# Vision tower on one core: the channel sums taken in two pieces a tile (three and four runs) instead of three (two, two, three), with the step tables laid out anew

## The reference

```
pooled = x.reshape(64, 12, 14, 16, 14, 16).sum(axis=(3, 5))
h = einsum('bcij,ce->bije', pooled, channel_weights)      # (64, 196, 192)
h = h + attn(layernorm(h))                                # one head of width 192
h = h + ffn(layernorm(h))                                 # 192 -> 768, gelu (tanh) -> 192
```

## Time and profile before

| | us |
|---|---|
| median of three runs | 494.9 (493.6 to 494.9) |
| the profiled execution | 494.9, of which span of the instructions 492.8 |
| PE busy | 425.7 |
| DVE busy | 381.7 (77% of the span) |
| ACT busy, POOL busy | 287.8, 255.0 |
| sums of pieces of two runs (96) and of three (48) | 190.4, 141.5 |

### The profile page before, as it was taken

How to read it: one execution, slowest core, us unless ns; L and a number is a source line. 1 busy time by engine, 2 the same in 40 slices (tenths; PEclk the granted TensorE clock), 3 DMA queues, 4 the chain that set the end, 5 groups by cost and what they waited for, 6 DMA issues and landing times.

```text
span 492.8 us, 10971 instructions
## 1 busy us (share of the span) xinstructions
PE 425.7 (86%) x4558; PEld 362.9 (74%) x4558; DVE 381.7 (77%) x288; ACT 287.8 (58%) x494; POOL 255.0 (52%) x194
## 2 busy tenths in 40 slices
PE   5976453996899999899898989798999899999996
PEld 4544232784678888788787978687888779888896
DVE  1788898899799998899989898989898999420000
ACT  1022044534878676758583858575868466877821
POOL 1032313703659293818374758475656657485940
PEclk9999555696699999989998999999999989999999
DMA  8999999999999999999999999999999997101101
GB/s 241 335 404 401 404 402 402 403 402 406 402 401 401 403 403 403 403 399 404 397 403 398 404 395 400 396 401 402 397 403 399 400 391 310 34 26 33 43 26 50
DMA packets 56661, 166.65 MB, mean 338 GB/s; under 512 B 5972, under 2 KB 13030, under 8 KB 56612
## 3 DMA queue, kind: packets, MB, share of 16 engines
q1 hardware_dynamic: 56612, 165.95, 87.7%
HBM read 156.29 MB, written 9.63 MB: 337 GB/s over the span
## 4 chain that ended last, share of the span: by engine, by line
DMA 47%; DVE 20%; PE 17%; SPq 7%; issue 4%; POOL 3%; ACT 1%; DVEq 0%; ACTq 0%
DMA xs<-x 47%; DVE pooled L480 18%; PE ps L609 17%; SPq L412 5%; POOL h_lo L1123 2%; DVE phat_tok L498 1%; POOL inv L1100 0%; POOL inv L1114 0%; ACT probs L967 0%; ACT out_sb L1024 0%; PE ps L786 0%; SPq L429 0%; DVE prod L489 0%; ACT h_hi L1018 0%; DVEq L475 0%
## 5 line engine op out<-in xcount | busy, mean ns | idle before, releaser
L480 DVE TENSOR_REDUCE pooled<-xs 128x28 f32<-128x1792 f32 x144 | 328.8, 2323 | 29.3 <-DMA xs<-x 29.3
L1123 POOL TENSOR_TENSOR h_lo<-h_f,h_hi 128x784 fp32r<-128x784 f32 x96 | 176.9, 1868 | 86.6 <-ACT h_hi L1018 86.6
L609 PE MATMUL ps<-w_hi,h_hi 128*98 128x192 f32 x768 | 207.9, 271 | 1.3 <-POOL h_lo L1123 1.1
L609 PE MATMUL ps<-w_lo,h_hi 128*98 128x192 f32 x768 | 196.9, 256 | 0.0
L609 PE MATMUL ps<-w_hi,h_lo 128*98 128x192 f32 x768 | 196.7, 256 | 0.0
L609 PEld LDWEIGHTS ps<-w_hi,h_hi 128*98 128x98 f32 x768 | 128.9, 168 | 16.7 <-issue 14.2
L609 PEld LDWEIGHTS ps<-w_lo,h_hi 128*98 128x98 f32 x768 | 129.4, 168 | 0.0
L609 PEld LDWEIGHTS ps<-w_hi,h_lo 128*98 128x98 f32 x768 | 129.1, 168 | 0.0
L1009 ACT ACTIVATE h_f<-ps 128x784 f32<-128x784 f32 x96 | 74.8, 824 | 21.7 <-PE ps L609 21.6
L1018 ACT CAST h_hi<-h_f 128x784 fp32r<-128x784 f32 x96 | 79.5, 851 | 0.1
L1100 POOL TENSOR_TENSOR inv<-var,minus_half 98x8 f32<-98x8 f32 x16 | 26.2, 1636 | 70.4 <-DVE var L494 70.3
(11 more groups left out here) (119 smaller groups left out, 355.4 us busy)
## 6 DMA issues: line engine op xcount, KB each, us to landing
xs<-x SPq DMA_DIRECT2D x336, 448.0 KB, 12.4
out<-out_sb SPq DMA_DIRECT2D x32, 294.0 KB
rows_sb<-wfc SPq DMA_DIRECT2D x1, 576.0 KB, 5.5
out_sb<-wproj SPq DMA_DIRECT2D x1, 576.0 KB, 10.4
h_f<-wqkv SPq DMA_DIRECT2D x1, 432.0 KB
cf<-const_full SPq DMA_DIRECT2D x1, 264.0 KB, 3.0
h_f<-const_paired SPq DMA_DIRECT2D x1, 153.0 KB, 3.3
cr<-const_rows SPq DMA_DIRECT2D x1, 83.2 KB
```

Of the source, the lines that this page charges most:

```text
L480: dve.tensor_reduce(pooled[:, n % 2, t, GRID * first:GRID * end].rearrange("p (i j) -> p i j", j=GRID), runs, AX.XY, ALU.add).then_inc(red ...
L609: return pe.matmul(o, a, b, start=start, stop=stop, skip_group_check=shared)
L1123: pool.tensor_tensor(h_lo[:, m % 2, t], h_f32[:, t], h_hi[:, m % 2, t].bitcast(F32), ALU.subtract).then_inc(h_lo_ready, 1)
```

## The change

The piece list has two entries instead of three. What depends on it follows: the number of pieces a group is six, DVE has 96 sums of `pooled` instead of 144, and the ring is given back in threes and fours.

```diff
-CHUNKS = ((0, 2), (2, 4), (4, 7))
+CHUNKS = ((0, 3), (3, 7))
 PER_TILE = len(CHUNKS)
 PER_GROUP = TILES * PER_TILE
...
 PERIOD = 254
-STEPS = 4910
+STEPS = 4938
...
-    "sum_rows": (443, 398, 375, 382, 391, 389, 367, 357, 353, 347, 337, 326, 316, 319, 313, 327),
+    "sum_rows": (365, 352, 347, 345, 333, 334, 365, 337, 341, 338, 326, 317, 311, 312, 334, 326),
...
 SETUP_AT = {
-    "pe_resid": 335, "pe_f": (389, 416), "pe_w1": (457, 494),
-    "act_f": 447, "act_w1": (476, 505), "dve_resid": 383,
-    "pool_wproj": 385, "pool_w1": 517,
+    "pe_resid": 335, "pe_f": (393, 420), "pe_w1": (462, 498),
+    "act_f": 452, "act_w1": (480, 510), "dve_resid": 387,
+    "pool_wproj": 385, "pool_w1": 522,
 }
```

More of the change, by code:

```diff
@@ L70 @@
 PERIOD = 254
-STEPS = 4910
+STEPS = 4938
 PE_ORDER = {
-    "sum_rows": (443, 398, 375, 382, 391, 389, 367, 357, 353, 347, 337, 326, 316, 319, 313, 327),
[L74 to L82, removed]
+    "sum_rows": (365, 352, 347, 345, 333, 334, 365, 337, 341, 338, 326, 317, 311, 312, 334, 326),
+    "turn_phat": (447, 420, 492, 431, 423, 414, 446, 394, 411, 392, 383, 375, 366, 365, 398, 408),
+    "apply_a": (476, 433, 505, 455, 489, 488, 508, 513, 491, 502, 494, 485, 477, 416, 421, 464),
+    "scores": (505, 564, 519, 543, 559, 553, 568, 553, 551, 542, 534, 525, 539, 510, 478, 480),
+    "turn_maxima": (567, 647, 646, 637, 604, 625, 609, 621, 611, 603, 594, 585, 588, 549, 544, 520),
+    "turned_scores": (581, 683, 659, 652, 618, 641, 639, 635, 627, 618, 609, 601, 602, 563, 570, 534),
+    "weigh": (613, 719, 700, 686, 650, 682, 671, 669, 660, 652, 643, 634, 633, 599, 637, 565),
+    "turn_context": (633, 744, 734, 715, 730, 709, 705, 692, 694, 686, 677, 669, 662, 630, 660, 598),
+    "turn_u": (647, 814, 772, 761, 753, 758, 764, 742, 744, 735, 727, 718, 701, 672, 687, 616),
+    "apply_g2": (660, 827, 823, 775, 778, 785, 781, 768, 770, 762, 753, 745, 726, 690, 705, 640),
@@ L83 @@
     "residual": (
-        (724, 850, 1043, 1039, 1028, 1022, 1018, 1008, 998, 987, 972, 961, 939, 930, 903, 838),
-        (1000, 1163, 1159, 1155, 1149, 1145, 1134, 1124, 1113, 1103, 1089, 1080, 1040, 1050, 1007, 923),
+        (665, 832, 1047, 1053, 1031, 1027, 1014, 1016, 1007, 999, 990, 998, 1000, 964, 949, 884),
+        (906, 1136, 1182, 1160, 1159, 1134, 1146, 1137, 1128, 1120, 1119, 1129, 1094, 1097, 1053, 969),
     ),
-    "turn_uhat": (784, 865, 821, 798, 799, 810, 799, 790, 779, 752, 747, 738, 716, 735, 704, 645),
+    "turn_uhat": (702, 885, 873, 838, 854, 836, 860, 836, 827, 819, 810, 802, 783, 741, 754, 691),
@@ L120 @@
 ACT_ORDER = {
[L121 to L125, removed]
+    "load_exp": (360, 574, 458, 560, 556, 546, 573, 558, 556, 548, 539, 530, 510, 514, 465, 478),
@@ L126 @@
+    "copy_p_tok": (375, 372, 357, 377, 365, 344, 375, 347, 351, 348, 336, 327, 321, 322, 358, 361),
+    "copy_phat": (460, 428, 499, 450, 442, 426, 459, 429, 425, 417, 408, 400, 376, 377, 410, 434),
+    "copy_b": (496, 442, 514, 537, 545, 543, 562, 547, 545, 536, 528, 519, 534, 426, 433, 474),
+    "copy_maxima": (576, 656, 654, 646, 613, 634, 618, 630, 620, 612, 603, 594, 597, 558, 553, 528),
     "exponentials": (
-        (609, 711, 655, 609, 603, 604, 605, 601, 584, 574, 563, 552, 532, 526, 535, 499),
@@ L128 @@
-        (617, 719, 663, 617, 611, 612, 613, 609, 592, 582, 571, 560, 540, 534, 543, 507),
-    ),
[L130 to L134, removed]
@@ L135 @@
-    "gelu": (
[6 rows of a table removed]
+        (595, 696, 673, 665, 632, 654, 652, 648, 640, 631, 623, 614, 615, 576, 584, 547),
+        (603, 704, 681, 673, 640, 662, 660, 656, 648, 639, 631, 622, 623, 584, 592, 555),
+    ),
+    "load_gelu": (611, 943, 935, 902, 924, 922, 918, 910, 901, 893, 887, 888, 851, 854, 817, 733),
+    "copy_context": (628, 732, 723, 700, 724, 695, 686, 682, 674, 665, 657, 648, 649, 619, 652, 587),
+    "copy_u": (654, 821, 810, 770, 762, 775, 776, 758, 758, 749, 740, 732, 720, 684, 699, 624),
@@ L142 @@
+    "keep_u": (658, 825, 829, 781, 774, 794, 788, 777, 769, 760, 752, 743, 732, 690, 707, 628),
+    "copy_uhat": (710, 892, 880, 846, 861, 844, 868, 843, 835, 826, 818, 809, 791, 752, 763, 703),
+    "gelu": (
[6 rows of a table added]
     ),
     "round_high": (
[6 rows of a table removed]
[6 rows of a table added]
     ),
     "take_out": (
[4 rows of a table removed]
[4 rows of a table added]
     ),
@@ L159 @@
     "reduce": (
[9 rows of a table removed]
[6 rows of a table added]
     ),
-    "variance1": (486, 416, 428, 421, 413, 440, 398, 420, 412, 404, 368, 362, 354, 355, 358, 346),
+    "variance1": (391, 380, 460, 399, 387, 375, 405, 353, 371, 355, 343, 335, 328, 329, 362, 365),
     "maxima": (
-        (561, 663, 538, 558, 550, 543, 535, 527, 520, 512, 507, 499, 475, 476, 477, 443),
-        (571, 673, 548, 568, 560, 552, 545, 537, 529, 522, 517, 509, 484, 485, 486, 453),
-    ),
-    "context": (695, 787, 710, 673, 659, 687, 679, 671, 664, 657, 651, 614, 604, 607, 614, 557),
-    "variance2": (750, 831, 784, 747, 740, 762, 754, 746, 739, 704, 696, 689, 670, 691, 656, 611),
+        (546, 597, 604, 592, 580, 572, 588, 576, 590, 578, 569, 563, 564, 523, 520, 493),
+        (556, 636, 614, 602, 590, 582, 598, 586, 600, 588, 579, 572, 573, 533, 530, 503),
+    ),
+    "context": (640, 807, 765, 753, 742, 716, 749, 699, 712, 700, 692, 687, 688, 661, 666, 604),
+    "variance2": (668, 851, 839, 788, 818, 796, 822, 798, 786, 774, 766, 767, 739, 698, 714, 648),
 }
 POOL_ORDER = {
-    "scale_p": (493, 423, 442, 428, 438, 457, 405, 437, 433, 421, 376, 369, 362, 371, 372, 362),
-    "scale_u": (760, 841, 796, 771, 771, 781, 769, 765, 753, 727, 720, 713, 684, 704, 676, 621),
+    "scale_p": (419, 387, 467, 406, 394, 382, 413, 361, 378, 363, 351, 342, 336, 337, 370, 373),
+    "scale_u": (678, 860, 848, 809, 828, 809, 833, 811, 803, 794, 786, 777, 756, 708, 723, 658),
     "low_part": (
[6 rows of a table removed]
[6 rows of a table added]
     ),
@@ L191 @@
     "load": (
[9 rows of a table removed]
[6 rows of a table added]
     ),
     "send": (
-        (1089, 1254, 1247, 1246, 1226, 1223, 1225, 1215, 1204, 1194, 1174, 1168, 1131, 1140, 1098, 1014),
-        (1195, 1388, 1379, 1369, 1363, 1359, 1349, 1339, 1328, 1317, 1302, 1284, 1275, 1245, 1183, 1099),
+        (976, 1209, 1255, 1233, 1231, 1207, 1219, 1210, 1201, 1193, 1190, 1202, 1162, 1170, 1126, 1042),
+        (1082, 1374, 1380, 1358, 1351, 1341, 1341, 1332, 1323, 1315, 1325, 1327, 1290, 1274, 1211, 1127),
     ),
```

## The result

The changed kernel takes 499.25 us (499.11 to 499.63, four runs) against 494.9 (493.6 to 495.65) for the kernel before on the same chip. These medians differ by 4.35 us, a ratio of 1.0088. The ratio on record is 1.0114, with a 95% interval of 1.0093 to 1.0134; it is not that of these medians but fits a kernel before of about 493.7 us. By either the changed kernel is slower, by about 1%. The forecast was 498.1, with a range of 494.6 to 500.8. Against these, which were timed apart from the changed kernel, the change costs 5.6 to 6.2 us.

A forecast was written before the change was run, and what follows sets the result against it. Input was taken to set the pace until group 14's `sum_rows` at 397.25 us, then PE's queued work. A longer last sum (0.94) plus work moved behind it (2.28) put 3.2 us on 494.9: 498.1 us, range 494.6 to 500.8.

The forecast's parts named there:

- hinge: Group 14's `sum_rows` at 397.25 us, taken as the last wait for input, with 95.5 us of PE work behind it.
- the half-clock stretch: PE's granted clock at 0.50 between 399 and 402 us, right after the 1.20 us wait, said to cost 1.7 us.
- A later wait?: Check of group 15's `sum_rows`: PE there at 423.8 us, the last piece done at 423.5, so no wait.
- No wait, but with nothing to spare: Verdict on group 15's `sum_rows`: its last piece ends 0.3 us ahead of PE.
- the seven units: Four `project`s, `residual`, `hidden` and `weigh`, moved behind group 15's `sum_rows`, about 4.1 us, bringing PE there earlier.
- Group 14's terms (+0.94, +2.28): At group 14's `sum_rows`: last sum ends 0.94 us later (one run longer), 2.28 us more PE work behind it.
- these three units: `hidden`, `weigh` (1.75 us together) and a `project` (0.53 us), moved from ahead of group 14's `sum_rows` to behind it.
- The sign I had named: `sum_rows` of group 14 starting at 398.1 to 398.4 us, behind a PE wait longer than 1.2 us.
- another step: The step on PE's order at group 14's `sum_rows`, where `hidden` and `weigh` were priced at 1.75 us.
- DVE the bound: Rival: DVE sets the pace, so its 6.3 us saving comes through in full, 488.6 us; chance 0.06.
- PE runs the tail without its slow stretch: Rival: the slow clock between 399 and 402 us does not come, 1.7 us less, 496.4 us; chance 0.16.
- The hinge isn't a hinge: Rival: PE's total work sets the end, late groups' waits only shift, the time stays at 494.9 us; chance 0.11.

The follow-up runs named there:

- e3_before_fill: The kernel before with group 14's `sum_rows` put behind the `residual`, `turn_context` and two `project`s that followed it: 492.99 us, ratio 0.9992.
- e4_tail_fill: The changed kernel with `maxima` of group 14 earlier and group 15's `sum_rows` behind a `residual`, two `project`s and a `hidden`: 497.26 us, ratio 1.0082.
- e5_last_split: The changed kernel with group 15's four-run pieces summed and given back as two and two: 498.30 us, ratio 1.0093.
- e12_sums_later2: The changed kernel with `sum_rows` of groups 9 to 15 and the chain behind them put later, `maxima` of group 14 earlier: 496.95 us, ratio 1.0070.

## Why the prediction was right, and where it was not

- **The model was right, its hinge was not.** The end is the last gate plus the work behind it. I took group 14's `sum_rows` for the gate because PE had waited there, and group 15's for free because it had not. In that execution PE was 1.7 us late at group 15's, as much as the half-clock stretch costs; e3_before_fill, without wait and stretch, has it right behind the piece. The step that failed is the one headed "A later wait?", with its "No wait, but with nothing to spare": it took the seven units only as time by which PE comes earlier, and put them at nothing in the sum. With nothing to spare there, the gate is there as soon as anything ahead of it gets shorter.
- **Group 14's terms (+0.94, +2.28).** The piece ended at 398.07 (398.04 worked out) and `sum_rows` stood at 398.57, PE late by 0.5. But these terms did not reach the end as they stand. As I read the profile, they were taken up by the 1.32 and 0.74 us waits at 420 and 424; no run puts these three units back by themselves, so this is argued and not shown. The sign I had named, a wait longer than 1.2 us in front of that `sum_rows`, did not come: it had none, and it started later than the 398.1 to 398.4 I gave.
- **What took their place.** The units behind group 15's `sum_rows`: 69.19 - 64.44 = 4.75 us. I had listed these seven units and priced them at 4.1, `residual` at 0.4 where it takes 0.8, `hidden` and `weigh` at 1.6 though another step had 1.75. The rest is the gate itself: group 15's last piece ends 1.2 us later (424.19 for 422.97). 4.75 + 1.2 = 6.0 us is what a kernel before that waits at that gate should lose, and its medians on the three chips of the experiments give 5.6 to 6.2. (Its estimated gate of 423.1 was worked out from such a median, so that figure is no second witness.) Against the profiled execution of 494.9 it is 4.75 less 0.34 for the gate (424.33 for 424.67), 4.4 us: there PE had come 1.7 us late to the gate, and now it comes in time, which hides the later piece.
- **The end of input.** I had it near 416 us, from the row of slices. It was at 419.50 in the kernel before already, and is at 420.17 now. The DMA is full until 412 us and thins out after that (179 GB/s from 416 to 417, 43 from 419 on), so the row of slices shows the end of the full stream and not the last landing. I also gave the last matmul's end as 489.6, which is the end of ACT's copy; it is 489.10 before and 493.52 after, 4.4 us later and not 3.
- **DVE.** The 6.3 us I expected it to save were worth nothing to the end, as costed, and only 2.7 of them show in DVE's busy time (379.0, forecast about 375), since sums in a row overlap. "DVE the bound" (488.6 us) is refuted.
- **"PE runs the tail without its slow stretch"** came true in part: the clock is 1.00 from 398.5 on. It earned little at the end, since most of the 1.7 us turned up as waits at the gate. I had counted it as a full gain because it lay behind the (wrong) hinge.
- **"The hinge isn't a hinge"** was right about group 14 and wrong about the time.

The forecast of 498.1 thus came close by luck: its 3.2 us were terms at the wrong gate, and the 4.4 to 6 us that were lost are others. That the gate is group 15's rests on e3_before_fill for the kernel before, and on the wait and the chain in the profile for the changed one. e4_tail_fill and e5_last_split fit it, the one by moving little else than what stands around group 15's `sum_rows`, the other by opening that gate 0.7 us earlier; by themselves they would also fit a sum that starts at group 14 and counts the later waits.

## What to carry to other kernels

In a kernel with a fixed order that goes from input-bound to PE-bound, look for the last instruction that needs input, waited for or not, and count the work queued behind it. Work that an edit moves behind it costs its full time; work that was only shifted ahead of it cost and earned nothing that could be measured (e3_before_fill, e12_sums_later2), as long as PE still reached the gate in time. A gate without a wait in one trace may have one in the next execution, so bound its spare time before you call it free.
